# Slot comparison one tile at a time, narrower numbering products, and no idle TensorE products in the heads of two expert layers

## The reference

```
x = x + 0.5 * ffn(layernorm(x))
x = x + attention(layernorm(x))        # 16 heads of 8, rotary, causal
x = x + 0.5 * ffn(layernorm(x))
```

## Time and profile before

| what | value |
|---|---|
| median of 3 runs | 790.07 us (789.43 to 792.0) |
| time of the profiled execution | 789.8 us |
| its span, first to last instruction | 788.1 us |
| TensorE busy (products) | 750.8 us, 95% of the span |
| VectorE busy | 600.0 us, 76% |
| ScalarE busy | 505.5 us, 64% |
| GpSimd busy | 322.6 us, 41% |
| head of layer 0 | about 0 to 45 us |
| head of layer 1 | about 653 to 692 us |

### The profile page before, as it was taken

One profiled execution on the slowest core, in us unless ns is written; L12 is line 12 of the kernel. 1 busy time (PEld: TensorE's weight loads), 2 busy tenths in 40 slices (PEclk: granted clock), 3 DMA queues, 4 the chain that ended last, 5 costly groups with the idle time before them and its releaser, 6 DMA issues. The chain is left out here.

```text
span 788.1 us, 17158 instructions
## 1 busy us (share of the span) xinstructions
PE 750.8 (95%) x5299; PEld 400.6 (51%) x5299; DVE 600.0 (76%) x1871; ACT 505.5 (64%) x1221; POOL 322.6 (41%) x609
## 2 busy tenths in 40 slices
PE   9989999898999999999999999999999998999994
PEld 7468897554433333333333333333333454378894
DVE  5566775499898988889888888888898756456663
ACT  3056663386357787788788878887888770066662
POOL 6077755156522234223432332343235310176743
PEclk9899999999999999999999999999999999699997
DMA  9722111227551452244234414542351011321110
GB/s 286 296 50 51 54 43 44 101 63 191 149 92 31 87 90 61 43 95 93 70 63 96 85 47 68 122 79 54 61 101 63 15 36 47 113 54 46 53 35 28
DMA packets 36654, 64.14 MB, mean 81 GB/s; under 512 B 10456, under 2 KB 22104, under 8 KB 35160
## 3 DMA queue, kind: packets, MB, share of 16 engines
q1 hardware_dynamic: 30472, 53.59, 28.3%
q0 software_dynamic: 4096, 8.69, 4.1%
q10 hardware_dynamic: 2000, 0.80, 0.4%
HBM read 39.58 MB, written 23.09 MB: 80 GB/s over the span
## 5 line engine op out<-in xcount | busy, mean ns | idle before, releaser
L1556 DVE CUSTOM_DVE_ANT_0 cst<-psS,mask_row 128x768 bf16<-128x768 f32 (+7 forms) x512 | 359.9, 754 | 48.9 <-PE psS L1407 46.1
L1519 ACT ACTIVATE prob<-psST 128x512 f32<-128x512 f32 (+3 forms) x750 | 321.5, 494 | 97.9 <-PE psST L1457 59.5
L1472 PE MATMUL a_psO<-prob,vs 128*32 128x512 f32 (+3 forms) x1536 | 159.1, 496 | 0.0
L1679 POOL TENSOR_TENSOR a_gate<-a_zeros 1x1 f32<-1x1 f32 x128 | 23.5, 183 | 265.3 <-ACT prob L1519 264.9
L1457 PE MATMUL psST<-a_qs,ks 75*128 75x512 bf16 (+1 forms) x480 | 126.3, 328 | 0.0
L1407 PE MATMUL psS<-ks,a_qs 72*128 72x512 bf16 (+2 forms) x480 | 114.2, 326 | 0.2 <-DVE a_rowmax L1556 0.2
L812 POOL DMA_INDIRECT tok<-rows,f_there_number x64 | 61.9, 968 | 82.5 <-DVE f_number L511 37.4
L1457 PEld LDWEIGHTS psST<-a_qs,ks 75*128 75x128 bf16 x480 | 41.5, 96 | 99.0 <-ACT prob L1519 69.0
L1680 POOL TENSOR_SCALAR_AFFINE_SELECT prob<-prob 128x512 f32<-128x512 f32 x128 | 80.0, 625 | 0.0
L1457 PE MATMUL psST<-qs,ks 75*128 75x512 bf16 (+3 forms) x270 | 72.0, 328 | 0.2
L1407 PE MATMUL psS<-ks,qs 72*128 72x512 bf16 (+3 forms) x288 | 68.8, 327 | 0.7 <-DVE a_rowmax L1556 0.3
(11 more groups left out here) (196 smaller groups left out, 1023.4 us busy)
## 6 DMA issues: line engine op xcount, KB each, us to landing
sums<-p_anT SPq DMA_DIRECT2D x30, 256.0 KB, 4.3
a_qs<-q_split SPq DMA_DIRECT2D x60, 96.0 KB
rows<-tok SPq DMA_DIRECT2D x8, 536.0 KB, 4.8
ks<-k_split SPq DMA_DIRECT2D x32, 128.0 KB
qs<-q_split SPq DMA_DIRECT2D x36, 96.0 KB
q_split<-p_part SPq DMA_DIRECT2D x24, 128.0 KB, 2.4
k_split<-p_part SPq DMA_DIRECT2D x24, 128.0 KB, 2.4
ks<-k_split SPq DMA_DIRECT2D x16, 192.0 KB
```

Source lines behind the costliest of these rows:

```text
L1472: last = nc.tensor.matmul(psO[32 * h:32 * h + 32, c0:c0 + w], vs[r][:, j, h, :], prob[:, u % RING, h, 0:w], start=(j == 0), stop=(u + 1 in ...
L1519: nc.scalar.activation(prob[:, u % RING, h, 0:w], score_buffer(s, u * QH + h)[:, 0:w], ACT.Exp, scale=SCALE).then_inc(exp_done, 1)
L1556: last = nc.vector.tensor_tensor_reduce(out=out[:, a * CH:a * CH + width], in0=ps[:, a * CH:a * CH + width], in1=mask_row[:, S - width:], ...
```

## The change

The slots are compared one tile at a time, 32 instructions with a per-token scalar in place of 4 with two tensors, into rows in which the 128 values of one tile lie side by side. [...] TensorE waits for each tile's comparison by itself. The product reads its 64 columns once and not three times. All idle products behind the logits are dropped, in both layers; `IDLE_FIRST` stays.

```diff
 IDLE_FIRST, IDLE_LOGITS, IDLE_CHOICE, IDLE_RANKS, IDLE_NUMBERS, IDLE_ITEMS, IDLE_LAST = (
-    20, (0, 0, 0, 0, 0, 0, 0, 0), (14, 40), 2, 20, (4, 10), 5)
-LOGITS_WIDE, NUMBERS_WIDE = 14, 3
+    20, (0, 0, 0, 0, 0, 0, 0, 0), (0, 0), 0, 0, (0, 0), 0)
+LOGITS_WIDE = 14
...
-for _name, _width in (("before", P), ("slot", P * TB), ("tile", NT * NT), ("column", NT),
+for _name, _width in (("before", P), ("slot", P), ("tile", NT * NT), ("column", NT),
...
-    put("slot", np.repeat(i, TB))
+    put("slot", i)
...
-        slot, tile = (sb(k, [P, NT], BF16) for k in ("slot", "tile"))
+        slot, tile = sb("slot", [P, NT]), sb("tile", [P, NT], BF16)
...
-        slot_is = spare[:, 0:NT * P].rearrange("p (q k t) -> p q k t", k=P, t=TB)
+        slot_is = spare[:, 0:NT * P].rearrange("p (t k) -> p t k", k=P)
...
-                for q in range(NT // TB):
-                    nc.vector.tensor_tensor(slot_is[:, q, :, :],
-                                            slot[:, q * TB:(q + 1) * TB].unsqueeze(1).to_broadcast([P, P, TB]),
-                                            fixed("slot", a=P, b=TB), ALU.is_equal).then_inc(slots_found, 1)
-                    if q == 0:
-                        dve.wait_ge(tiles_found, 1)
-                        nc.vector.tensor_tensor(tile_number[:, 1, :, :], tile_is,
-                                                fixed("column").unsqueeze(1).to_broadcast([P, NT, NT]),
-                                                ALU.mult).then_inc(low_made, 1)
+                nc.vector.tensor_scalar(slot_is[:, 0, :], fixed("slot"), slot[:, 0:1], None,
+                                        ALU.is_equal).then_inc(slots_found, 1)
+                dve.wait_ge(tiles_found, 1)
+                nc.vector.tensor_tensor(tile_number[:, 1, :, :], tile_is,
+                                        fixed("column").unsqueeze(1).to_broadcast([P, NT, NT]),
+                                        ALU.mult).then_inc(low_made, 1)
+                for t in range(1, NT):
+                    nc.vector.tensor_scalar(slot_is[:, t, :], fixed("slot"), slot[:, t:t + 1], None,
+                                            ALU.is_equal).then_inc(slots_found, 1)
...
-                pe.wait_ge(slots_found, t // TB + 1)
-                last = nc.tensor.matmul(psM, slot_is[:, t // TB, :, t % TB],
-                                        tile_number[:, :, :, t].rearrange("p k s -> p (k s)").unsqueeze(1)
-                                        .to_broadcast([P, NUMBERS_WIDE, 2 * NT]),
+                pe.wait_ge(slots_found, t + 1)
+                last = nc.tensor.matmul(psN, slot_is[:, t, :],
+                                        tile_number[:, :, :, t].rearrange("p k s -> p (k s)"),
                                         start=(t == 0), stop=(t == NT - 1))
```

More of the change, by code:

```diff
@@ L352, in ffn @@
         psN = number_ps[:, 2 * P:2 * P + 2 * NT]
-        psM = number_ps[:, 2 * P:2 * P + NUMBERS_WIDE * 2 * NT].rearrange("p (k c) -> p k c", k=NUMBERS_WIDE)
         psW = spare_ps[:, :]
```

## The result

The changed kernel took 781.55 us, the median of 4 runs (780.71 to 782.78), against 790.88 (789.43 to 792.0) for the kernel before: a ratio of 0.9884, with a 95% interval of 0.9861 to 0.9908. That is 9.3 us faster. The profiled execution took 782.78 us with a span of 781.1; against the span before of 788.1 that is 7.0 us.

The account below looks back on a forecast made before the run. The head was taken as one thread of engines waiting in turn, TensorE's work nearly alone on the path. Layer 1's -8.15 and layer 0's -4.7 sum to -12.85 us, giving 777.2 us, range 773.8 to 781.8.

Parts of the forecast that it names:

- the price of a comparison: VectorE's 31 comparisons of 128 values: 0.105 us each assumed, range up to 0.205, so done at 676.1, before TensorE's products.
- Numbering products: 32 TensorE products giving tokens their numbers: 0.11 us each instead of 0.333, so numbers come 7.0 us earlier in each layer.
- The small row: Profile row of two independent 32-value VectorE instructions starting 0.10 us apart, from which the comparison's 0.105 us was taken.
- the three instructions on `whole`: Small VectorE instructions queued behind the comparisons; claimed to end at 676.7, before TensorE's last result at 677.2.
- VectorE becomes the bound: Rival, 12%: comparisons at one value per cycle, 0.205 us each, end after TensorE's products and delay the numbers: 781.0 us.
- Gather in layer 0: Gather of rows after the numbers: held by late stores until about 34.1 instead of 40.63, so -6.5 us.
- Idle ahead of the experts: Dropping idle products before the first expert transpose lets it start earlier: -2.5 us in layer 1, -0.3 in layer 0.
- Projection: Layer 1's projection: without 5 idle products between its halves, the second half ends earlier, -1.25 us.
- Ranks: Rank products after the projection run at lower clock without idle products: +0.5 us in layer 1, +0.25 in layer 0.
- Clock in the experts: First experts start at half clock until it returns after some 5 us: +2.0 us in each layer.
- the bounds of 1.0 to 4: Range for the first experts' clock loss: at least 1.0 us, 4 if the clock takes 9 us to return.
- The prediction's own terms for the idle products: Terms from dropping idle products: projection, ranks, wait before the transpose, and low clock plus slower transpose (+2.1 in each layer).

Follow-up runs that it names:

- e3: The changed kernel unaltered, run again on another chip for a second profile: 782.48 us, ratio 0.9926.
- e6: The changed kernel, but TensorE starts its numbering products only after all 32 comparisons, and VectorE runs 48 extra unread instructions of eight forms in layer 0: 795.63 us.
- e5: The kernel before, with numbering products reading the 64 columns once; its comparison and idle products kept: 776.01 us, ratio 0.9839.
- e10: The kernel before with 64 columns read once and the idle products behind the logits dropped, old comparison kept: median 780.38 us, ratio 0.9889.
- e2: The changed kernel with all the old idle products put back: 781.44 us, ratio 0.9907.
- e1: The kernel before with only the idle products behind the logits dropped: 793.11 us, ratio 1.0059.
- e4: The changed kernel with the 64 columns read three times again, 192 columns against contiguous weights: 793.22 us, one run.
- e7: The kernel before with 64 columns, and 10 idle products directly behind the numbering products, none behind the wait for the items: 777.76 us, ratio 0.9856.
- e11: The kernel before, unaltered, one run for a second profile: 787.43 us.
- e12: The changed kernel unaltered, one run for a third profile: 780.75 us.
- e8: The changed kernel with 10 idle products directly behind the numbering products and no others behind the logits: 778.99 us, ratio 0.9868.

## Why the prediction was right, and where its sizes were off

The sign and the path of the gain came out, and the range, narrowly and with some luck: on the chip of `e3` the same kernel took 782.48 us, outside it. The step that failed in size is the price of a comparison, taken at 0.105 us and measured at 0.162. Point by point:

- **Numbering products, predicted -7.0 us in each layer; measured -5.75** (L474 to `numf`: 9.77 us against 15.52, and in layer 0 9.78 against 15.51). The speed-up of TensorE was right: 0.110 us a product where nobody holds it up (`e6`), against the 0.11 taken, and by the columns at 1.7 ns each, as reasoned from the row. The step that was mis-sized is "I take 0.105, nearest to the 0.10 of the small ones": a comparison costs 0.162 us. The small row was of an instruction with a constant; the scalar operand per token costs 0.06 us more, and `e6` shows both. In the forecast's own times, 672.83 + 31 x 0.162 = 677.85 and not 676.1, so behind TensorE's 677.2; and the three instructions on `whole`, thought "still in time", then stand between the last comparison and `numf`: in the profile after 0.53 us lie between them (676.73 to 677.26), while the last product had ended at 677.06. 684.28 - 677.85 - 0.53 is 5.9, near the measured 5.75. So the rival "VectorE becomes the bound" is the mechanism that happened, at a price between the two. The reason given for it, one value a cycle, was wrong: a value costs 0.25 ns (`e6`), and only the fixed part is large. The Trainium skill's formula ("VectorE: DVE Perf Modes", The TRN2 errata), which gave 94 ns, is near the 103 of the form with a constant and short of the 165 with the per-token scalar. The Trainium skill's warning there against small tiles held in this case.
- **Gather in layer 0, predicted to lose 0.5 us to the stores.** In the changed kernel it lost nothing, since the numbers came only at 34.31: the gather began 1.29 us later, as before. `e5`, whose numbers come at 32.31, shows that the limit is real and at the place given.
- **Idle ahead of the experts: -2.5 and -0.3 predicted, -2.37 and -0.24 measured** (xn's end to the transpose: 0.14 us against 2.51 in layer 1).
- **Projection: -1.25 predicted.** The two profiles give 2.94 against 4.89 us from its start to the second half, -1.95, because the clock was full there in the one and low in the other. It varies between executions of one kernel: from the projection to the ranks before took 14.32 and 12.64 us, after 12.35, 13.14 and 12.35. With low clock in both it is 13.14 - 14.32 = -1.2, with full clock in both -0.3.
- **Ranks: +0.5 and +0.25 predicted, +0.32 and +0.21 measured** (L650 to `f_tri` 1.55 and 1.44 us, 1.23 before).
- **Clock in the experts: +2.0 in each layer predicted; in layer 1 +2.65 and in layer 0 +2.8 measured** (first to third `hidden` 6.54 us against 3.89, and 6.71 against 3.89), and in layer 0 0.3 more between the transpose and the first `hidden`. By the windows the clock came back 6.3 and 6.9 us after the first of them, not 5, and in the other two profiles 5.9 to 8.2 us (the 8.2 in layer 1 of `e3`). Both costs are within the bounds of 1.0 to 4.
- **Not predicted: attention takes 2.5 us longer, 1.7 of it the dip.** No step of the sum looked past the third item. From the third `hidden` of layer 0 to the start of layer 1 it takes 604.2 and 603.7 us in the two profiles of before and 606.7, 607.0 and 606.5 in those of the changed kernel. What is not the dip is not explained.

The measured terms of layer 1 add up: -1.95 + 0.32 - 5.75 - 2.37 + 2.65 = -7.10, and the profiles give -7.08. The forecast had -8.15. In layer 0 the terms give 0.21 - 5.73 - 0.24 + 0.3 + 2.82 = -2.6 where -4.7 was forecast; then come the later start (+0.5) and attention (+2.5, with the dip), and the stretch behind layer 1's third `hidden` is 0.3 shorter: -7.1 - 2.6 + 0.5 + 2.5 - 0.3 = -7.0. The start and the dip are no cost of the change that the runs settle: between kernels and executions the ranks of layer 0 start anywhere from 22.0 to 23.5 us.

**What the prediction did not see** is how the parts stand to each other, which the runs show. With 64 columns in all four, the ratios to the kernel before are:

| | idle products kept | idle products dropped |
|---|---|---|
| comparison of before | 0.9839 (`e5`) | 0.9889 (`e10`) |
| new comparison | 0.9907 (`e2`) | 0.9884 and 0.9926 (the changed kernel, `e3`) |

Each has an interval of 0.2 to 0.3% to either side. 64 columns alone give -1.6% (`e5`, 12.1 us by the medians, 12.7 by the ratio). So the whole gain comes from the product that reads its columns once. Dropping the idle products costs 0.6% in the kernel before (`e1`, 5 us) and 0.5% in `e5` (`e10`, 3.9 us), but nothing clear of noise beside the new comparison. The new comparison costs 0.7% where the idle products stay (`e2` against `e5`, 5.4 us, of which their profiles show 3.2 in the two heads), and 1.1 us in each layer by the profiles of `e10`, which its whole time doesn't resolve; the forecast had nothing for it. Neither of the two edits gives a gain clear of noise in any pair of kernels, and their costs do not simply add. The prediction's own terms for the idle products, never added up there, are -1.25 + 0.75 - 2.5 - 0.3 + 2.1 + 2.1 = +0.9 us; the runs say +4 to +5 with the comparison of before.

**Still open.** What decides the dip at 155 us: it was in the three profiles of the changed kernel (154 to 160), in `e2` and `e5` (151 to 158), and in none of the two of before, `e1`, `e4`, `e6` to `e10`. The wait ahead of it was 2.22 us in all of them. `e7` to `e10` too end layer 0 earlier than before and have no dip, so the earlier end alone doesn't bring it. `e5` has the dip and is still among the fastest. Why `e2` is not faster than the changed kernel beyond its 10 slow idle products was not tested; its profiled execution, the slowest of its six, had the projection of layer 1 at low clock. Against `e11`, the second profile of before, `e1` loses 3.2 us up to the third `hidden` of layer 0, 1.2 in attention, 1.0 in layer 1 and 0.1 behind it, which make the 5.5 us between their spans (791.2 and 785.7); why attention takes 1.2 us more is open.

## What to carry to other kernels

Price each edit of a combined change by itself, and sum a filler together with the clock that it buys: here one edit made the whole gain, and the two others together gave some of it back. A product whose moving operand is strided pays by its columns, so take columns away before making the weights contiguous. When an engine is sped up, ask at once whether its feeder, at its real spacing and not that of a similar-looking instruction, keeps pace, and what stands in the feeder's queue behind it.

## What the runs showed of the hardware

- A VectorE instruction with a scalar per token costs 0.06 us more than with a constant: 0.165 against 0.103 us from start to start, both on 128 values, both for `is_equal` and (L520 and L519) for a product. Its recorded duration, 0.25 us, is not its price in a row of them, 0.162.
- A moving column at a stride of 64 bytes costs 1.67 ns, with either kind of weights. The pace is the same at 2.4 and at 1.2 GHz: 0.328 us a product on both sides of the fall before, 0.114 in `e5` and in `e10`. Weights at a stride of 16 bytes cost 0.005 us more for a product.
- TensorE busy in every record does not hold the clock. In the kernel before it falls to 1.2 GHz within products that leave no gap, at 32 and 677 us. In the changed kernel it was low already when the numbering products began (granted 0.50 in each window from 28 to 46 us) and took 6.9 and 6.3 us of experts to come back (5.9 to 8.2 in `e3` and `e12`), with waits of 0.64 us among them. In `e8`, 10 idle products begun at 675.09 had it back within the window at 678. A wait can undo that: in `e7` it fell in the window at 38, behind 2.95 us without products.
